# A gated recurrence solved by sweeps: gate sums kept in PSUM, slopes kept from the fourth sweep, the state updated in place

## What is computed

```python
Wh, Wz = W[:, :D], W[:, D:]
leak = 1.0 - alpha
def step(h, z_t):
    gate = sigmoid(h @ Wh.T + z_t @ Wz.T + b)
    h_new = tanh(h * leak + gate * z_t)
    return (h_new, h_new)
_, hs = lax.scan(step, h_t, swapaxes(z, 0, 1))
```

## Time and profile before

| | |
|---|---|
| median of 3 runs | 1064.97 us (1064.23 to 1065.26) |
| the profiled execution | 1066.98 us |
| its span in the profile | 1065.0 us |
| busy in the span | PE 762.8, DVE 661.0, ACT 501.4, POOL 257.4 us |
| mean granted TensorE clock | 0.83 |
| the sweeps, first gate sum to last scan | 653.2 to 803.6 us of the span |

### The profile page before, as it was taken

How to read it: one execution, slowest core, us unless ns; L and a number is a source line. 1 busy time by engine, 2 the same in 40 slices (tenths; PEclk the granted TensorE clock), 3 DMA queues, 4 the chain that set the end, 5 groups by cost and what they waited for, 6 DMA issues and landing times. The chain is left out here.

```text
span 1065.0 us, 15050 instructions
## 1 busy us (share of the span) xinstructions
PE 762.8 (72%) x5686; PEld 469.3 (44%) x5686; DVE 661.0 (62%) x953; ACT 501.4 (47%) x824; POOL 257.4 (24%) x231
## 2 busy tenths in 40 slices
PE   4720008979866367784974749999992779999995
PEld 1310003325645356762532424444442556676673
DVE  4999946873654888357667652999993413333331
ACT  5878734540423333554542326999991203223221
POOL 0000000000102000000332401988982023433431
PEclk9965558975798858897976869999995569999997
DMA  6600010000494000002000019000003911111100
GB/s 227 230 23 0 0 49 2 0 1 0 136 262 116 3 2 22 3 3 92 1 0 1 1 39 376 1 1 1 0 1 100 335 34 40 40 48 38 36 16 0
DMA packets 35514, 60.64 MB, mean 57 GB/s; under 512 B 8028, under 2 KB 22492, under 8 KB 34755
## 3 DMA queue, kind: packets, MB, share of 16 engines
q1 hardware_dynamic: 29826, 51.27, 14.9%
q0 software_dynamic: 3312, 6.31, 2.0%
q10 hardware_dynamic: 2304, 2.10, 0.6%
HBM read 55.20 MB, written 7.21 MB: 59 GB/s over the span
## 5 line engine op out<-in xcount | busy, mean ns | idle before, releaser
L1826 ACT ACTIVATE moe_ht<-x_tr,moe_b 128x128 f32<-128x128 f32 x184 | 50.1, 383 | 147.6 <-PE x_tr L1791 147.5
L1782 PE MATMUL x_y<-moe_w,moe_ht 128*128 x368 | 85.0, 385 | 2.1 <-ACT moe_ht L1826 2.1
L1773 PE MATMUL x_hid<-w,moe_xt 128*128 x184 | 85.7, 610 | 0.9 <-DVE moe_xt L1916 0.7
L1105 POOL TENSOR_TENSOR path<-path,mix_pr 128x1280 f32<-128x1280 f32 x16 | 38.3, 2422 | 155.4 <-DVE mix_pr L1267 155.4
L1782 PEld LDWEIGHTS x_y<-moe_w,moe_ht 128*128 128x128 f32 x368 | 69.4, 193 | 11.6 <-issue 2.8
L1923 DVE COPY moe_hid<-x_hid 128x512 f32<-128x512 f32 x46 | 31.8, 691 | 64.6 <-PE x_hid L1773 44.1
L205 PE MATMUL bad_sum<-spike_bad,ones 128*128 128x16 f32 x2 | 0.6, 386 | 88.7 <-ACT spike_outside L171 88.7
L1435 PE MATMUL r_bank<-recur_h_other,recur_wg 128*128 128x512 f32 x128 | 60.2, 592 | 0.0
L1431 PE MATMUL r_bank<-recur_zw,eye 128*128 128x512 f32 x112 | 57.2, 592 | 0.8 <-ACT recur_zw L1466 0.8
L201 PE MATMUL w_bank<-spike_wbuf,spike_pick 128*128 128x512 f32 x80 | 39.2, 649 | 21.4 <-DMA spike_wbuf<-in_gW 21.4
L369 PE MATMUL pj<-hs,proj_wqkv 128*128 128x512 f32 x96 | 45.5, 623 | 12.6 <-DMA mix_st<-in_c_spread 12.6
(11 more groups left out here) (277 smaller groups left out, 1872.6 us busy)
## 6 DMA issues: line engine op xcount, KB each, us to landing
spike_wbuf<-in_gW SPq DMA_DIRECT2D x8, 1280.0 KB, 6.3
w<-in_w1T SPq DMA_DIRECT2D x8, 1024.0 KB, 12.6
moe_w<-in_w2T SPq DMA_DIRECT2D x8, 1024.0 KB, 10.9
fir_band<-in_band_l SPq DMA_DIRECT2D x11, 512.0 KB
xT<-in_xT SPq DMA_DIRECT2D x4, 1024.0 KB, 6.6
fir_band<-in_band_m SPq DMA_DIRECT2D x11, 312.0 KB
mix_st<-in_band_l SPq DMA_DIRECT2D x5, 512.0 KB
z_rows<-recur_change SPq DMA_DIRECT2D x8, 256.0 KB, 3.1
```

What stands on the lines that cost most here:

```text
L1105: nc.gpsimd.tensor_tensor(x, x, w, ALU.mult).then_inc(s.weighted, 1)
L1773: last = nc.tensor.matmul(hid_bank[n][:], xt[:, c, :], m.w1[:, bass.ds(e, 1), c, n * N:(n + 1) * N].rearrange("p o n -> p (o n)"), start=( ...
L1782: last = nc.tensor.matmul(y_bank[:], ht[:, k, :], w2[:, bass.ds(e, 1), k, :].rearrange("p o n -> p (o n)"), start=(k == 0), stop=(k == K2 ...
L1826: nc.scalar.activation(ht[:, k, :], tr_bank[k // (K2 // 2)][:, k % (K2 // 2) * P:(k % (K2 // 2) + 1) * P], ACT.Relu, bias=b1[:, bass.ds(e, ...
```

## The change

- Each of the eight units has a PSUM bank of its own, and its gate sum stays there through all sweeps. The first sweep adds Wh times the first guess to the Wz z that the bank holds already; each later sweep adds Wh times the *change* of the sweep before. The product with the identity is gone. The bias goes into the sigmoid.
- With all eight banks taken, the gate (a new ring of four, `gate`) and the slopes (`slopes`, one for each unit) lie in SBUF.
- Slopes are formed in the first four sweeps only (`SLOPES`); sweeps five to seven use those of the fourth.
- The state is updated in place in `m.h`; `change` gets the state's layout, with a first column of zeros.
- The rows on their way to DRAM lie in `rest`, and the wait for their transfer moves from DVE to POOL.

The functions of the recurrence, with helper and name lines left out:

```diff
-    SWEEPS, TOL = 7, 1.6e-5
+
+
+    SWEEPS, SLOPES, TOL = 7, 4, 1.6e-5
...
-        other = sb("h_other", [P, J, 1 + T])
+        gate = sb("gate", [P, 4, N])
+        slopes = sb("slopes", [P, UNITS, N])
         step = sb("step", [P, UNITS, N])
         rest = sb("rest", [P, UNITS, N])
-        change = sb("change", [P, UNITS, N])
+        change = sb("change", [P, J, 1 + T])
...
-        state = (other, m.h)
         RING = 4
-        a_bank = bank[:RING]
-        j_bank = bank[RING:]
...
+            return x[:, (c if k is None else k) * B + b, t0:t0 + N]
...
+        def at(x, u):
...
+            return x[:, c * B + b, 1 + t0:1 + t0 + N]
...
-                             change[:, i, :].rearrange("p (a n) -> p a n", n=D)).then_inc(s.rows_out, 16)
+                             rest[:, i, :].rearrange("p (a n) -> p a n", n=D)).then_inc(s.rows_out, 16)
...
-            pe.wait_ge(s.zw_ready, UNITS)
-            pe.wait_ge(s.leaks, 5)
+            pe.wait_ge(s.leaks, 4)
             for u in range(ALL):
-                b, t0, c = unit(u)
-                out = a_bank[u % RING][:]
-                if u >= RING:
-                    pe.wait_ge(s.f_ready, u - RING + 1)
-                nc.tensor.matmul(out, m.eye[:], zw[:, c * B + b, t0:t0 + N], start=True, stop=False)
-
-                pe.wait_ge(s.h_ready, u - u % C + C)
+                c = u % C
+                if u < UNITS:
+                    pe.wait_ge(s.zw_ready, u + 1)
+                    pe.wait_ge(s.h_ready, u - c + C)
+                else:
+                    pe.wait_ge(s.g_ready, u - UNITS + 1)
+                    pe.wait_ge(s.change_ready, u - UNITS - c + C)
+                    pe.wait_ge(s.zeroed, 1)
+                x = m.h if u < UNITS else change
                 for k in range(C):
-                    last = nc.tensor.matmul(out, wg[:, k, c * P:(c + 1) * P],
-                                            state[u // UNITS % 2][:, k * B + b, t0:t0 + N], start=False,
-                                            stop=(k == C - 1))
+                    last = nc.tensor.matmul(bank[u % UNITS][:], wg[:, k, c * P:(c + 1) * P], shifted(x, u, k), start=False,
+                                            stop=(k == C - 1), skip_group_check=True)
                 last.then_inc(s.a_psum, 1)
...
             def sigmoid(u):
+                c = u % C
                 act.wait_ge(s.a_psum, u + 1)
-                nc.scalar.activation(a_bank[u % RING][:], a_bank[u % RING][:], ACT.Sigmoid).then_inc(s.g_ready, 1)
+                nc.scalar.activation(gate[:, u % RING, :], bank[u % UNITS][:], ACT.Sigmoid,
+                                     bias=bias[:, c:c + 1]).then_inc(s.g_ready, 1)
 
             def value(u):
                 act.wait_ge(s.u_ready, u + 1)
-                nc.scalar.activation(step[:, u % UNITS, :], a_bank[u % RING][:], ACT.Tanh).then_inc(s.f_ready, 1)
+                if u >= UNITS:
+                    act.wait_ge(s.res_ready, u - UNITS + 1)
+                nc.scalar.activation(step[:, u % UNITS, :], gate[:, u % RING, :], ACT.Tanh).then_inc(s.f_ready, 1)
 
             def slope(u):
                 c = u % C
-                out = j_bank[u % RING][:]
-                if u >= RING:
-                    act.wait_ge(s.change_ready, u - RING + 1)
+                out = slopes[:, u % UNITS, :]
+                if u >= UNITS:
+                    act.wait_ge(s.change_ready, u - UNITS + 1)
                 act.wait_ge(s.f_ready, u + 1)
...
-                    slope(u - LAG_F)
+                    if u - LAG_F < SLOPES * UNITS:
+                        slope(u - LAG_F)
...
+            nc.gpsimd.memset(change[:, :, 0], 0.0).then_inc(s.zeroed, 1)
             pool.wait_ge(s.h_ready, UNITS)
+            pool.wait_ge(s.rows_out, 16 * UNITS)
 
             def residual(u):
                 pool.wait_ge(s.f_ready, u + 1)
-                nc.gpsimd.tensor_tensor(rest[:, u % UNITS, :], step[:, u % UNITS, :], at(u),
+                if u >= UNITS:
+                    pool.wait_ge(s.h_ready, u + 1)
+                nc.gpsimd.tensor_tensor(rest[:, u % UNITS, :], step[:, u % UNITS, :], at(m.h, u),
                                         ALU.subtract).then_inc(s.res_ready, 1)
 
             def move(u):
                 pool.wait_ge(s.change_ready, u + 1)
-                nc.gpsimd.tensor_tensor(after(u), at(u), change[:, u % UNITS, :], ALU.add).then_inc(s.h_ready, 1)
+                nc.gpsimd.tensor_tensor(at(m.h, u), at(m.h, u), at(change, u), ALU.add).then_inc(s.h_ready, 1)
...
-            dve.wait_ge(s.rows_out, 16 * UNITS)
...
             def argument(u):
                 b, t0, c = unit(u)
-                x = a_bank[u % RING][:]
+                x = gate[:, u % RING, :]
                 dve.wait_ge(s.g_ready, u + 1)
                 nc.vector.tensor_tensor(x, x, m.xT[:, c * B + b, t0:t0 + N], ALU.mult).then_inc(s.gz_ready, 1)
                 dve.wait_ge(s.gz_ready, u + 1)
-                nc.vector.scalar_tensor_tensor(x, before(u), leak[:, c:c + 1], x, ALU.mult, ALU.add).then_inc(s.u_ready, 1)
+                if u >= UNITS:
+                    dve.wait_ge(s.h_ready, u + 1)
+                nc.vector.scalar_tensor_tensor(x, shifted(m.h, u), leak[:, c:c + 1], x, ALU.mult, ALU.add).then_inc(s.u_ready, 1)
 
             def solve(u):
                 b, t0, c = unit(u)
                 r = u % UNITS
-                first = 0.0 if t0 == 0 else change[:, r - C, N - 1:N]
-                dve.wait_ge(s.j_ready, u + 1)
+                first = 0.0 if t0 == 0 else change[:, c * B + b, t0:t0 + 1]
+                if u < SLOPES * UNITS:
+                    dve.wait_ge(s.j_ready, u + 1)
                 dve.wait_ge(s.res_ready, u + 1)
                 if t0:
                     dve.wait_ge(s.change_ready, u - C + 1)
-                nc.vector.tensor_tensor_scan(change[:, r, :], j_bank[u % RING][:], rest[:, r, :], first,
+                dve.wait_ge(s.a_psum, min(u - c + (C if t0 else 2 * C), ALL))
+                nc.vector.tensor_tensor_scan(at(change, u), slopes[:, r, :], rest[:, r, :], first,
                                              ALU.mult, ALU.add).then_inc(s.change_ready, 1)
...
```

More of the change, by code:

```diff
@@ L1529, in _ @@
                 dve.wait_ge(s.turned, i + 1)
[L1530 removed]
+                nc.vector.tensor_copy(rest[:, i, :], bank[i][:]).then_inc(s.turned_out, 1)
             dve.wait_ge(s.w_in, W_IN)
```

18 lines of the change are left out of this document (5 added, 13 removed).

## The result

| | before | after |
|---|---|---|
| median of 3 runs, us (lowest to highest) | 1064.97 (1064.23 to 1065.26) | 1163.40 (1163.03 to 1164.02) |
| profiled execution, us / its span | 1066.98 / 1065.0 | 1163.40 / 1161.6 |
| first DVE operation of the sweeps, us | 658.17 | 657.73 |
| end of the last scan, us | 803.6 | 900.7 |

The ratio is 1.0927, with an interval of 1.0902 to 1.0951: 98.4 us slower by the medians, 96.4 by the two profiled executions. The forecast was 1164.0. The last scan ends 97.1 us later, so the whole difference arises in the recurrence; what follows is 0.7 us shorter.

The account below looks back on a forecast made before the run. PE was taken as the bound at 2.573 us per unit, DVE close behind. First operation at 656.5, plus 5.1, 54 x 4.40 = 237.6 and 3.4, put the last scan at 902.6, +99.0: median 1164.0, range 1139 to 1190.

Parts of the forecast that it names:

- What bounds it before: Recurrence sweeps: PE sets the pace at 2.573 us per unit, with DVE right behind at 2.54.
- The turns: Recurrence: DVE operations with two SBUF inputs and POOL's operations wait for each other; 512 columns hold DVE's turn 0.54 us.
- the rival in which only tensor_tensor does: Recurrence: only DVE's first operation waits for POOL, about 3.3 us per unit, 1102 us in all; chance 0.07.
- The rival with no turns at all: Recurrence: DVE runs at its 2.54 us per unit and becomes the bound, 3.4 us less, 1061.6; chance 0.05.
- The unit: One unit of the recurrence: 2.16 us of DVE's turns, 2.10 of POOL's and 0.14 of handover, 4.40 together.
- the handover from DVE to DVE: From DVE's second operation to the scan: the start isn't hidden, 0.14 us per unit.
- The bounds of 4.02 and 4.81: Us per recurrence unit: 4.02 if POOL held its turn only for its per-column part, 4.81 if nothing overlapped.
- no overlap at all: Rival, recurrence: DVE's and POOL's starts also fall outside each other's turn, 4.81 us per unit, 1186 us; chance 0.10.
- The signs: New profile: DVE's first two operations about 1.6 us, scan near 1.22, DVE and POOL always busy, PE idle over half.
- The sum: Recurrence: first DVE operation 656.5, then 5.1, 237.6 and 3.4 us; last scan ends at 902.6, +99.0.
- Two short iterations: Start of the recurrence: the first two iterations lack scan and POOL operations, 2.55 us each, 5.1 together.
- The added waits: Recurrence: new waits of DVE, ACT and PE cost zero, with PE some four units ahead as cover.

Follow-up runs that it names:

- e9: The kernel before with only the change's start: in the first four units sigmoid bias, no identity product, no wait for the last zw; 1062.81 us against 1067.65, ratio 0.9949.
- e1: The kernel before with only the gate in SBUF, so DVE's first two operations have two SBUF inputs; 1139.32 us, beside 1063.03 for before.
- e2: The kernel before with only the slopes in SBUF, so only the scan has two SBUF inputs; 1100.79 us, beside 1063.03 for before.
- e6: The kernel before with the product with z written to SBUF, so only DVE's second operation reads two SBUF tensors; 1082.12 us, beside 1064.63 for before.
- e4: The changed kernel with POOL's residual and move replaced by memsets, which read nothing; 1061.58 us, beside 1063.03 for before.
- e7: The changed kernel with new slopes in all seven sweeps instead of four; 1161.63 us.
- e8: The changed kernel with a product of the identity and a tile of zeros added on PE for every unit; 1159.55 us.
- e5: The kernel before with the gate in SBUF and its product with z written to the bank: only DVE's first operation has two SBUF inputs; 1070.05 us, before 1064.63.
- e11: The gate-in-SBUF kernel of e1 with residual, scan and move one iteration later; 1105.58 us, beside 1069.68 for before.
- e10: The changed kernel with POOL's residual and move replaced by copies with one SBUF input each; 1142.12 us, beside 1067.65 for before.
- e3: The changed kernel with POOL's residual and move given to DVE; 1125.21 us, 38.2 less than the changed kernel.

## Why the prediction was right, step by step

**What bounds it before.** Right, and e9 bears it out: with PE ahead by four products, DVE fell from 2.569 to 2.536 us a unit, so DVE's slack of 0.03 was real, and the stage lost 1.9 us where DVE's pace over 56 units gives 1.8. One reason given for PE's pace was the wrong way round: a missing record would make the spacing shorter than 0.427 us, not longer. The 2.573 itself is good to 0.004, by DVE's starts.

**The turns.** The central step held. It was read from a handful of stretched additions in another stage, for one form of instruction. The second form and the scan take turns as well (e1, e2, e6), so the rival in which only tensor_tensor does falls. The rival with no turns at all falls with the 1.5 us of the first two operations. Where there are no turns, in e4, the stage does run like before's, so that rival's condition was the right one; but its price was wrong. It gave DVE's pace of 2.54 and ACT as harmless, and with slopes e4's units take 2.66 us with ACT full. By the length of e4's stage (1.6 us more than before's, where the rival had 1.8 less) its 1061.6 was too low by some 3 us. That e4 took 1061.58 in all is luck: its first operation came at 654.5, 3.7 us earlier than in before, of which the changed start explains only 1.6 to 1.8.

**The unit: 4.40 forecast, 4.343 measured.** By the ends in the two timelines above, a unit holds DVE's two turns of 0.54 to 0.56, one of 1.12 for the scan, POOL's move of 1.12 and its residual of 1.08 or 0.89 (700.43 to 701.32). That sums to some 4.33, and the scans with a carry take a little more. The forecast had 2.16 for DVE, 2.10 for POOL and 0.14 for the handover from DVE to DVE. The last was the mis-sized term: DVE's second operation ends at 703.54 and the scan is recorded from 703.45, so its start does pass beside the operation ahead. The two turns and the scan together take 2.22, not 2.30. (The 0.07 us by which the second operation is longer were put down to a pointer operand. No run takes the pointer away; the ends show only that nearly all of it lies outside the turn, 0.56 beside 0.54.) The bounds of 4.02 and 4.81 were each off by more than 0.3 us, and no overlap at all is excluded.

**The signs.** The durations came as foretold, 1.55, 1.61 and 1.21 us for DVE's three, and so did the same pace with slopes and without. Two signs did not. POOL was to seem busy all the time, but is recorded busy for 70%: it waits 1.29 us for the tanh in each unit, beside the scan, which the prediction's own order of a unit implies. And PE was to be idle over half of the time, but was so for only 41 and 48%, since its matmul records grew from 0.592 to 0.789 us. Neither bears on the pace.

**The sum.** Four terms, against the forecast of the last scan's end at 902.6, which came at 900.7:

- 53 units, 0.057 us less each: -3.0.
- Two short iterations: 4.27 us in place of 5.1: -0.8. The second sigmoid was ready early, and the third was what DVE waited for.
- The first operation came at 657.7, not at 656.5: +1.2. The step itself was sound. In the trace of after all of this stage began late (the first tanh at 639.77 us, before at 638.41), and from there the start is 1.8 us shorter, against 1.6 forecast.
- The tail from the last first operation on: 8.6 in place of 7.8: +0.8.

That makes about -1.9; another 0.7 us went behind the recurrence, and the profiled execution came to 1163.4 against 1166.0. The medians agree to 0.6 us (1163.4 and 1164.0) only because before's profiled execution stood 2.0 above its own median and after's stands at it. So the closeness of the total is partly luck; the closeness of the unit, 1.3%, is the part that was earned.

**What was worth nothing.** The kept slopes (e7) and the product with the identity (e8) were costed at zero, with their cover named, and both are zero. ACT's work with slopes came to 2.68 us a unit (71.58 of 116, times 4.343), against "at most 2.6": its operations on SBUF were under-priced by some hundredths each, which here 4.3 us hide. The added waits weren't tried apart; but e1, without them, shows the same stretched operations.

**The expectations of the runs** fared worse than the prediction. e5 and e6 missed (0.15 and 0.19 us of pace where 0.5 and 0.9 stood), for they took POOL's phase over from e1 instead of asking where POOL finds room. e1 came out dearer than its sum of turns for the reverse reason. What decides whether POOL falls into the phase of e1 or that of e5 was seen (it waits for the tanh, or it doesn't), and e11 shows that the lag of the residual sets it; why e1's loop stays in the poor phase while e6's doesn't is left open.

## What to carry to other kernels

Before an operand moves from PSUM to SBUF, count the SBUF inputs of every VectorE operation that reads it and look at what GpSimd does at that time: two such inputs beside a GpSimd operation that reads SBUF turn two engines that overlap into one queue, and the unit costs at least the sum of its turns, here 4.34 us in place of 2.57. The profile shows it beforehand, where any such pair already meets: durations of one group whose longest is far above the median, with ends that follow the other engine's. Where such pairs can't be avoided, try the work on one engine (3.71 us here), or put GpSimd's operations beside those of VectorE that have an input in PSUM.

## What the runs showed that I hadn't expected

- A POOL copy with one SBUF input takes turns as well as an operation with two (e10: 1.03 and 1.83 us for DVE's first two operations), and a fill doesn't (e4: 0.69 and 0.75).
- VectorE alone beat VectorE and GpSimd together, 3.71 against 4.34 us a unit, with five operations instead of three (e3: 705.12 less 701.41 us, from one first operation to the next).
- The granted clock of PE fell to 0.84 and 0.78 with PE busy for 59 and 52% of the time, and its matmuls took 0.79 us in the mean instead of 0.59. It cost nothing: PE was idle for the other 41 and 48%.
- ACT's operations became dearer with SBUF in place of a bank. Where the destination alone changed, in the first of the slope's two operations, the mean rose from 0.602 to 0.632 us (0.630 in e2). The Trainium skill, "ScalarE: Activation LUTs", section "Step-by-step: what each stage is for", says that an activation into PSUM is faster than one into SBUF; this pair agrees. Most of the sigmoid's rise from 0.58 to 0.67 is something else, though: without a bias pointer it takes 0.589 into SBUF (e1). And e4 shows that ACT can decide, for it set the pace there.
